# A transformer and state-space chain: set-up with block-diagonal folding ahead of the first block's stages, and another table of side steps

## The reference

```python
x = x + attn_a(layernorm(x))      # 16 heads, latent width 32, rotary, causal
x = x + ffn(layernorm(x))         # weights and activations through blockwise FP4
x = x + attn_b(layernorm(x))      # two directions of a selective scan, d_inner 512, d_state 16
x = x + ffn(layernorm(x))
```

## Time and profile before

| what | value |
| --- | --- |
| median of 3 executions | 4221.96 us (4219.04 to 4224.25) |
| the profiled execution, its own time | 4215.24 us |
| its span in the trace | 4213.5 us |
| PE busy | 3521.7 us, 84% of the span |
| DVE busy | 3054.1 us, 72% |
| ACT busy, POOL busy | 2036.8 us, 1927.2 us |
| first scan, last scan | 427.6 us, 4103.6 us |

### The profile page before, as it was taken

The page is one execution under the profiler, slowest core; times in us unless marked ns, Lnnn a source line. Parts: engine busy times, 40 slices in busy tenths (PEclk is TensorE's granted clock), DMA queues, the critical chain, the costliest instruction groups (busy, mean ns, idle before and its releaser), DMA issues.

```text
span 4213.5 us, 41483 instructions
## 1 busy us (share of the span) xinstructions
PE 3521.7 (84%) x13488; PEld 1871.2 (44%) x13488; DVE 3054.1 (72%) x4294; ACT 2036.8 (48%) x3852; POOL 1927.2 (46%) x1154
## 2 busy tenths in 40 slices
PE   5886798789988898879988899888988899879657
PEld 5553354245543454435543455434544355434214
DVE  3243768877687867877788776878678777887993
ACT  0354464635645455534655346544555346463441
POOL 0100744546444454445545464544544454453760
PEclk9997899999999999999999999999999999999998
DMA  3002544744446444364436444464454645364780
GB/s 84 1 1 79 190 148 130 248 166 159 142 139 237 143 142 165 137 231 138 152 133 214 157 162 147 143 233 137 136 167 147 220 143 156 128 219 145 268 275 5
DMA packets 203816, 649.64 MB, mean 154 GB/s; under 512 B 34253, under 2 KB 45520, under 8 KB 197456
## 3 DMA queue, kind: packets, MB, share of 16 engines
q1 hardware_dynamic: 203600, 646.98, 45.8%
HBM read 595.52 MB, written 51.38 MB: 154 GB/s over the span
## 4 chain that ended last, share of the span: by engine, by line
PE 48%; DVE 17%; issue 17%; ACT 11%; POOL 6%; SPq 1%; DMA 1%; POOLq 0%; DVEq 0%; ACTq 0%
PE banks L1268 18%; PE banks L1512 9%; DVE banks L844 7%; PE banks L1449 6%; PE banks L1297 5%; PE banks L1273 5%; ACT banks L1234 4%; DVE sb_arena L851 4%; PE banks L1425 3%; POOL sb_arena L980 3%; DVE sb_arena L772 2%; ACT sb_arena L1017 2%; SPq L427 1%; POOL sb_arena L892 1%; ACT sb_arena L1020 1%
## 5 line engine op out<-in xcount | busy, mean ns | idle before, releaser
L980 POOL TENSOR_TENSOR sb_arena<-sb_arena 128x1024 f32<-128x1024 f32 x512 | 1210.2, 2365 | 807.6 <-PE banks L1512 543.6
L844 DVE TENSOR_TENSOR_SCAN banks<-banks,sb_arena 128x512 f32<-128x512 f32 x1024 | 1197.9, 1215 | 212.3 <-ACT banks L1234 163.2
L1512 PE MATMUL banks<-sb_arena,sb_ident 128*128 128x512 f32 x2048 | 1041.0, 636 | 335.4 <-DVE sb_arena L851 266.0
L1234 ACT ACTIVATE banks<-sb_arena,sb_neg_a 128x512 f32<-128x512 f32 x1024 | 665.3, 682 | 1062.1 <-DVE sb_arena L851 1053.5
L1512 PEld LDWEIGHTS banks<-sb_arena,sb_ident 128*128 128x128 f32 x2048 | 386.6, 201 | 824.4 <-DVE sb_arena L851 434.1
L1017 ACT ACTIVATE sb_arena<-banks 128x512 f32<-128x512 f32 (+4 forms) x752 | 381.1, 519 | 582.8 <-PE banks L1273 389.1
L851 DVE TENSOR_TENSOR sb_arena<-banks,sb_arena 128x512 f32<-128x512 f32 x1024 | 650.5, 676 | 0.0
L1273 PE MATMUL banks<-sb_ident,sb_arena 128*128 128x128 f32 (+1 forms) x2082 | 343.8, 287 | 219.3 <-ACT sb_arena L1017 85.6
L1273 PEld LDWEIGHTS banks<-sb_ident,sb_arena 128*128 128x128 f32 (+1 forms) x2082 | 244.2, 145 | 429.7 <-ACT sb_arena L1017 156.7
L723 DVE TENSOR_REDUCE sb_nmax<-banks 128x1 f32<-128x512 f32 (+3 forms) x352 | 222.9, 636 | 290.9 <-PE banks L1452 289.4
L1449 PE MATMUL banks<-sb_arena 128*128 128x384 f32 (+3 forms) x1024 | 358.7, 461 | 0.7 <-issue 0.7
(11 more groups left out here) (126 smaller groups left out, 4027.3 us busy)
## 6 DMA issues: line engine op xcount, KB each, us to landing
sb_arena<-rows_bc SPq DMA_DIRECT2D x1024, 512.0 KB, 4.5
kept_xc<-sb_arena SPq DMA_DIRECT2D x16, 1024.0 KB, 5.0
kept_z<-sb_arena SPq DMA_DIRECT2D x16, 1024.0 KB, 4.4
sb_arena<-kept_z SPq DMA_DIRECT2D x64, 256.0 KB, 5.0
sb_arena<-kept_xc SPq DMA_DIRECT2D x64, 256.0 KB, 4.9
kept_zs<-sb_arena SPq DMA_DIRECT2D x8, 1024.0 KB, 6.6
sb_arena<-kept_zs SPq DMA_DIRECT2D x8, 1024.0 KB, 9.7
sb_xin<-in_x SPq DMA_DIRECT2D x8, 512.0 KB, 7.6
```

The lines of the kernel that those rows point to most:

```text
L844: v.tensor_tensor_scan(factors, factors, products, 0.0, ALU.mult, ALU.add).then_inc(V.sem, V.mark("scan", K, e))
L980: nc.gpsimd.tensor_tensor(dBu[K % SLOTS], u[:, p % 2].unsqueeze(1).to_broadcast([P, 2, T]), rows_b[K % BS], ALU.mult).then_inc(G.sem, G.ma ...
L1234: nc.scalar.activation(psum[:, e], dt[:, (K // NQ) % 2], ACT.Exp, scale=neg_a[:, s, m, 2 * q + e:2 * q + e + 1]).then_inc(A.sem, A.mark("d ...
L1512: mm = pe.matmul(psum[:, YB], ident[:, :], dBu[K % SLOTS][:, e], start=(q == 0 and e == 0), stop=(q == NQ - 1 and e == 1))
```

## The change

1. **Loads in three groups.** `fold_loads` (19: attention weights, identity, the small matrices and biases) on their own semaphore, issued first and without a wait for DVE's memsets; then x of block 0; then `mid_loads` (18: rotary tables, the FFN weights, mask, `w_qk`, `w_proj`), then the 19 left (`loads`: the scan layer's weights).
2. **Folding by block diagonals.** `wat` lies as 128 rows of 6 x 256. PE copies a small matrix to 8 heads' rows with `rep16`; DVE multiplies by a mask of heads (`heads_of`) and so makes block diagonals `bd[0]`, `bd[1]` (128 x 512) and `bdv` (128 x 128). Eight matmuls with 128 rows and 512 columns then give all of `w_lat`, four with 128 columns `w_v`. ACT copies each bank out in two pieces of 128 x 256.
3. **Stages of block 0 start earlier.** They are one generator, `front`, on each engine. DVE quantises a weight piece, takes 4 steps of `front`, and so on six times, then runs on to the end of attention; POOL likewise; ACT and PE run merge, latents and attention of block 0 first, and the turning of the FFN weights follows between attention and ffn1. `rates` and `neg_a` stand there too.
4. **The table** has new numbers in every stage. ffn1 has 11 half units instead of 12, prep ("early" and "late") 28 instead of 27; the sums of steps are as before.

```diff
 VISITS = {
...
-    "ffn1": (5, 2, 7, 9, 2, 5, 3, 4, 2, 6, 5, 3),
+    "ffn1": (3, 3, 15, 2, 6, 9, 5, 2, 5, 0, 3),
...
-        wat = area(3 * H, C, rows=HD)
+        wat = area(3 * CK, C)
...
         def _(sp):
+            for dst, src in fold_loads:
+                sp.dma_start(dst, src, allow_slow_non_contiguous=True).then_inc(s_fold, 16)
+            sp.dma_start(xin[:, :, :], x_dram[0]).then_inc(s_xin, 16)
             sp.wait_ge(V.sem, V.at("cleared"))
+            for dst, src in mid_loads:
+                sp.dma_start(dst, src, allow_slow_non_contiguous=True).then_inc(s_mid, 16)
             for dst, src in loads:
...
+            v.wait_ge(s_fold, FOLD)
...
+            for w in range(2):
+                v.wait_ge(E.sem, E.at("rep", w))
+                v.tensor_tensor(bd[w], psum[:, 1 + 6 * w, 0:2 * L].unsqueeze(1).to_broadcast([P, HPC, 2 * L]),
+                                heads_of.unsqueeze(2).to_broadcast([P, HPC, 2 * L]), ALU.mult
+                                ).then_inc(V.sem, V.mark("bd", w))
...
+            front = beside(None, 0)
+            advance(front, MERGE_N + 1)
+            v.wait_ge(s_mid, MID)
+            v.wait_ge(A.sem, A.at("w_v"))
             for i in range(3 * CK):
...
                 grid(qn_w[i % 2], qm_w[i % 2], "w", i)
-            v.wait_ge(A.sem, A.at("set_up"))
-            v.wait_ge(E.sem, E.at("set_up"))
-
-            drain(beside(None, 0))
+                advance(front, 4)
+            advance(front, LAT_N + ATT_N - 1 - 4 * 3 * CK)
+            v.wait_ge(s_w, LOADED)
...
+            drain(front)
...
             for w in range(2):
-                for r in range(2):
+                pe.wait_ge(V.sem, V.at("bd", w) if w == 0 else V.at("bdv"))
+                for h in range(2):
                     for k in range(CK):
...
+                        accumulate(psum[:, fold_bank(w, h, k)],
+                                   [(wat[:, CK * w + h, k * P:k * P + P], bd[w].rearrange("p h l -> p (h l)"))],
+                                   "w_lat", w, h, k)
...
+            pe.wait_ge(A.sem, A.at("w_v"))
+            pe.wait_ge(s_mid, MID)
+
+            front = beside(None, 0)
+            advance(front, MERGE_N + LAT_N + ATT_N)
             pe.wait_ge(G.sem, G.at("wq", 2 * CK - 1))
```

More of the change, by code:

```diff
@@ L1175, in beside @@
                     yield from prep(n)
+            a.wait_ge(s_fold, FOLD)
+            nc.scalar.activation(b_qk[:, :], b_qk[:, :], ACT.Copy, scale=SCALE).then_inc(A.sem, A.mark())
+            for w in range(2):
+                for h in range(2):
+                    for k in range(CK):
+                        a.wait_ge(E.sem, E.at("w_lat", w, h, k))
+                        for r in range(2):
+                            at = h * HPC * L
+                            copy(w_lat[w][r][:, k, at:at + HPC * L].rearrange("p (h l) -> p h l", l=L),
+                                 psum[:, fold_bank(w, h, k)].rearrange("p (h r l) -> p r h l", h=HPC, r=2)[:, r],
+                                 "w_lat", w, h, k)
+            for k in range(CK):
+                a.wait_ge(E.sem, E.at("w_v", k))
+                copy(w_v[:, k], psum[:, 3 + k, 0:C])
+            a.wait_ge(E.sem, E.at("b_lat"))
+            copy(b_lat[:, :], psum[:, 5, 0:4 * MT])
+            a.wait_ge(E.sem, E.at("b_v"))
+            copy(b_v, psum[0:1, 6, 0:C], "w_v")
+            front = beside(None, 0)
+            advance(front, MERGE_N + LAT_N + ATT_N)
             a.wait_ge(s_w, LOADED)
@@ L1541, in _ @@
             for h in range(H):
-                accumulate(psum[0:1, 3, h * HD:h * HD + HD], [(bq17[:, 2 * H + h:2 * H + h + 1], mt17)],
-                           *(("w_v",) if h == H - 1 else ()))
-            pe.wait_ge(G.sem, G.at("wq", 2 * CK - 1))
-            pe.wait_ge(A.sem, A.at("w_v"))
-            for i in range(2 * F // P):
-                for k in range(CK):
-                    last = i == 2 * F // P - 1 and k == CK - 1
-                    turn(psum[:, 3 * k + i // 4, (i % 4) * P:(i % 4) * P + P],
-                         rows_gu[:, i * C + k * P:i * C + k * P + P], *(("w_gu",) if last else ()))
+                accumulate(psum[0:1, 6, h * HD:h * HD + HD], [(bq17[:, 2 * H + h:2 * H + h + 1], mt17)],
+                           *(("b_v",) if h == H - 1 else ()))
@@ new lines, in _ @@
+            pe.wait_ge(A.sem, A.at("w_v"))
+            pe.wait_ge(s_mid, MID)
+            front = beside(None, 0)
+            advance(front, MERGE_N + LAT_N + ATT_N)
+            pe.wait_ge(G.sem, G.at("wq", 2 * CK - 1))
+            for k in range(CK):
+                for i in range(2 * F // P):
+                    c = i // 4
+                    if k >= 1 and i % 4 == 0:
+                        pe.wait_ge(A.sem, A.at("w_gu", k - 1, c))
+                    turn(psum[:, c, (i % 4) * P:(i % 4) * P + P], rows_gu[:, i * C + k * P:i * C + k * P + P],
+                         *(("w_gu", k, c) if i % 4 == 3 or i == 2 * F // P - 1 else ()))
@@ L1559, in _ @@
             pe.wait_ge(A.sem, A.at("set_up"))
-            accumulate(psum[0:17, 7, 0:1], [(e16[:, :], ones[0:1, 0:1])], "set_up")
-            drain(beside(None, 0))
+            pe.wait_ge(s_w, LOADED)
+            drain(front)
             for b in range(B):
```

147 lines of the change are left out of this document (79 added, 68 removed).

## The result

| what | before | after |
| --- | --- | --- |
| median of the runs on one chip | 4220.5 us (4218.95 to 4224.25, 4 runs) | 3990.24 us (3982.55 to 3990.97, 4 runs) |
| ratio, with its 95% interval | | 0.9449 (0.9433 to 0.9465) |
| the profiled execution, own time | 4215.24 us | 3982.55 us |
| start of the first unit's scans, of the last unit's | 427.6, 4102.5 us | 321.1, 3869.7 us |
| PE busy, DVE busy | 84%, 72% | 86%, 76% |

The changed kernel is 230 us faster, 106 more than forecast, and outside the range. Between the two profiled executions 106.6 us went ahead of the first scan (427.6 - 321.1), 126.2 between the scans of the first and the last of the 512 units (3674.8 to 3548.6), and nothing from there on (111.0, 111.1). So the set-up came out near its forecast (-101), and the table gave five times its -25.

The account below looks back on a forecast made before the run. Bounds taken: single engines waiting for each other in the set-up, PE in merge, latents and nearly attention, cross-engine chains in ffn2, ffn1 and prep. Set-up and block 0 -101, table -25: 4222.0 - 126 = 4096 us, range 4060 to 4140.

Parts of the forecast that it names:

- Set-up as a whole: Set-up and block 0: -111.7 for PE's earlier start, +6 and +5 given back, together -101 us; ends -84 and -108.
- Loads: Set-up: 0.79 us per issue, middle group as 38th issue at 31, landed at 32 us; ends 20 and 49.
- Folding: Set-up: new fold takes 13.4 us, from 13 to about 27, eight wide matmuls 6.6 of it, hidden behind the middle loads.
- The rival named after it: Set-up, fold at half clock: 10 us more, PE done at 37, five past the middle loads; 4101 us in all, chance 0.10.
- Quantising beside the latents: Block 0: DVE becomes the bound, full from 32 to 77; attention starts at 81 instead of 186.7, +6 us given back.
- Turning the FFN weights: Block 0, now between attention and ffn1: takes 8 us, less 3 that stand beside it, +5 us.
- The table: Loop stages: merge, latents and attention stay bound by PE, 0; ffn1, prep and ffn2 gain; seven blocks together -25 us.
- The spacing of ffn1, prep and ffn2: Loop: idle times there add up to 10 us per block; -3 per block taken, plus -0.7 for the moved half unit.
- The rival of all idle time gone: Loop: all idle time of the three places goes, -10 us per block; 4051 us in all, chance 0.12.
- The slower rival: Fifteen ffn1 steps between one unit's scans and hc idle DVE some 4.3 us, ffn1 stretches; about 4230 us, chance 0.03.
- Late loads: Set-up: middle loads land late, set-up and block 0 give -84 us; 4113 us in all, chance 0.10.
- the empty table: Loop: the new table of steps gives nothing, the set-up's -101 us remains; 4121 us in all, chance 0.20.

Follow-up runs that it names:

- e1: The changed kernel with the old table of steps in every stage, so the new set-up alone; 4116.73 us, ratio to before 0.9756.
- e8: The kernel before, with 200 bf16 matmuls of 512 columns added on PE while the loads are under way, ahead of the old fold; 4220.81 us.
- e12: e4's kernel, but in attention ScalarE alone takes both halves' steps ahead of the next unit's factors; 4009.92 us.
- e15: The changed kernel with its new table, ScalarE taking steps behind the hc ahead of the factors in attention alone; 3981.87 us, ratio 0.9435.
- e16: New set-up with the old table, ScalarE taking steps behind the hc ahead of the factors in attention alone; 4047.13 us, ratio 0.9591.
- e13: New set-up with the old table, ScalarE taking all side steps of a unit before the factors in every stage; 4149.62 us.
- e14: The changed kernel with its new table, ScalarE taking all side steps of a unit before the factors in every stage; 4151.18 us.
- e4: The changed kernel with attention's new numbers of steps per unit, all placed behind the unit's hc; 4207.12 us.

## Why the prediction was wrong, step by step

- **Set-up as a whole: right to 6 us, in part by luck.** Forecast -111.7, +6, +5, together -101, first scan 327. Its terms were off by -6.4, +4.9 and -3.5, and these misses offset each other in part. In the traces the gap to before is 118.1 at PE's first turn (143.68 to 25.56), 107.2 at the start of attention (186.7 to 79.5), 105.7 at ffn1's normalising (291.31 to 185.63) and 106.6 at the first scan. e1 has 104 by the medians.
- *Loads: sized too dear.* The 38 issues took 22.5 - 0.7 = 21.8 us, 0.57 each, not 0.79; the middle loads landed at 25.15 and not at 32. The range for this step (20 to 49) held it. (Its low end was reckoned wrongly: with PE held by the fold until 27 it is -106, not -108.)
- *Folding: right in its sum (13.4 against 13.0) by luck, wrong in its reading.* The wide matmuls took 9.2 us instead of 6.6, those ahead of 16 us at half clock; between the copies and them passed 0.2 instead of the 0.75 and most of the 1.5, and what follows them took 2.2 instead of 3.2. The forecast took 0.214 us per narrow record as full clock, because the window showed a granted clock of 1.00. The trace of before has its first clock record only at 129.4 us; ahead of it a window prints 1.00. e8, which has records there, shows 0.50, and the weight loads of before have the length of e8's at 0.50. In the changed kernel the rule that the forecast had set against the rows (the Trainium skill, TensorE: Matmul & The Clock Gate, "What's actually happening": an idle engine runs at half rate by default) holds: the fold starts at 0.86 us per record. The rival named after it was right in its mechanism, but it cost the wide matmuls 2.6 us and not some 7, as the clock rose at 16, and its 5 us in all did not come, since folding and normalising end at 25.4, where the middle loads land too.
- *Quantising beside the latents: 5 us more than forecast* (25.15 to 79.5 is 54.3, against 49), 1.5 of it a wait for GpSimd at the second piece that I had called gone, and PE's 43.55 for 39.65 at a granted clock of 0.91.
- *Turning the FFN weights: +1.5, not +5.* From the end of the projection to ffn1's normalising it is 4.85 us after (180.78 to 185.63) and 3.35 before (287.96 to 291.31).
- **The table: this is the step that failed.** It read "Merge, latents and attention keep PE as bound: 0, as what DVE gains there PE takes." For merge and latents it held (43.4, 49.6). For attention, with 143.66 of 158.00 us busy, it called "nearly" what left 14.3 us open, and did not ask what those were. 12.4 of them were waits of the transposes for ScalarE, and e12, e15 and e16 show that these depend on where a step stands against the factors: with ScalarE's order alone changed they fall to 3.0 (e16). Attention gave -62.5 of the -126.
- *The spacing of ffn1, prep and ffn2: right in kind, sized too small.* I took -3 of 10 idle us per block and -0.7; together these stages gave -65.8 over the loop, 9.4 per block. ffn1 at 67.6 came near its forecast of 67 (68.6 if cut at the hc's end), ffn2 came to 69.1 (71 to 72), prep to 82.9 (86 to 87). The rival of all idle time gone (-70) was nearly met in size, but not as it said: the first half unit of ffn1 still idles 2.53 us (1521.9 to 1524.45), 2.9 before, and in block 2 VectorE's idle time in the three stages fell from 36.0 to 29.8, while its busy time in them fell by another 3.3. Taking "nearest to a third" had no row behind it, and why the three stages gave this much is open.
- *The slower rival* did not come: under the fifteen steps of one unit VectorE idles 2.23 us, not 4.3, and ffn1 did not get longer. Late loads and the empty table are excluded by 25.15 us and by e1.
- *The range* followed from the sum: its low end 4060 took a strong table in three stages and nothing in attention. -101 - 70 - 62.5 would have been 3988.

## What to carry to other kernels

An engine that is busy 91% of a stage is no bound until the other 9% have a name: look up which instructions it idles ahead of, and who releases them. Where engines keep a fixed order and side work is dealt out in steps, a step costs by what the producer has ahead of it and the consumer has not; count these before moving numbers, and weigh a moved producer against what waits for the work it is put ahead of (e13, e14). Whether two parts of a change that touch different stretches add up is told by one run with each alone; here they did.

## What the chip showed that was not expected

- PE was busy 40.00 of 40.00 us at a granted clock of 0.50: so the back-to-back records of the old fold (16 rows, 32 columns) ran, although 45.7 us of wide matmuls had ended 3.3 us ahead of them (e8). The new fold, which turns to wide records 1.6 us after its start, went to full clock 6.1 us after its start.
- The granted clock of a window that lies ahead of a trace's first clock record reads 1.00 whatever the level was. The pitch of two equal weight loads tells the level in any stretch (here 0.86 or 0.43 us with 512 columns behind each, 0.21 or 0.11 with 32).
- PE's own busy time in attention of block 2 goes with the granted clock: 143.66 us at 0.98 before, 140.67 at 1.00 after, 152.43 at 0.93 in e4 with its 28.5 us of waits before the transposes. The sum of the waits alone doesn't tell the clock: e12 has 143.51 at 0.98 with 8.7 us idle in all, the changed kernel 8.3 idle at 1.00.
